# One decoder layer on one core: the conv taps of two units crossed on VectorE, and the scan's state made without a turn

## The reference

```python
xBC = causal_depthwise_conv(xBC, conv_w, conv_b)   # 4 taps over tokens, 4352 channels
...                                                 # x: 32 heads x 8; Bm, Cm: 32 heads x 64
CB = einsum('bcqhn,bckhn->bchqk', C, B)             # per chunk of 128 tokens and head
y_intra = einsum('bchqk,bckhp->bcqhp', CB * decay, xdt)
states = einsum('bckhn,bckhp->bchpn', B * state_decay[..., None], xdt)
new = carry * cd[:, :, None, None] + st             # state carried from chunk to chunk
y_inter = einsum('bcqhn,bchpn->bcqhp', C * exp(cum)[..., None], prev)
out = einsum('bli,oi->blo', y * silu(z + z_bias), W_out)
```

## Time and profile before

| | us |
|---|---|
| median of 3 runs (408.05 to 409.56) | 409.38 |
| profiled execution | 407.46 |
| its span | 405.7 |
| PE busy in the span | 381.7 (94%) |
| PE weight loads | 293.6 (72%) |
| DVE busy | 333.0 (82%) |
| ACT busy | 227.4 (56%) |
| POOL busy | 176.5 (43%) |

### The profile page before, as it was taken

How to read it: one execution, slowest core, us unless ns; L and a number is a source line. 1 busy time by engine, 2 the same in 40 slices (tenths; PEclk the granted TensorE clock), 3 DMA queues, 4 the chain that set the end, 5 groups by cost and what they waited for, 6 DMA issues and landing times.

```text
span 405.7 us, 8807 instructions
## 1 busy us (share of the span) xinstructions
PE 381.7 (94%) x2975; PEld 293.6 (72%) x2975; DVE 333.0 (82%) x564; ACT 227.4 (56%) x422; POOL 176.5 (43%) x208
## 2 busy tenths in 40 slices
PE   2998999999999999997899999899999999999996
PEld 1776776766767667665666676568888888888886
DVE  5798899999999999997889949748958759696685
ACT  7756555565564655657766731584554545546541
POOL 3897411101111011105536750235586755867561
PEclk9999999999999999998999999999999999999999
DMA  7302221322220122214231150000102020100003
GB/s 207 92 6 53 65 62 36 87 57 62 62 56 16 54 61 63 59 30 115 61 95 40 47 159 10 2 0 2 56 23 78 2 78 9 69 2 0 2 1 105
DMA packets 35932, 21.13 MB, mean 52 GB/s; under 512 B 17048, under 2 KB 33760, under 8 KB 35904
## 3 DMA queue, kind: packets, MB, share of 16 engines
q1 hardware_dynamic: 35904, 20.78, 18.4%
HBM read 18.13 MB, written 1.31 MB: 48 GB/s over the span
## 4 chain that ended last, share of the span: by engine, by line
PE 67%; DVE 15%; ACT 7%; issue 6%; POOL 2%; DMA 1%; ACTq 0%; DVEq 0%; SPq 0%; POOLq 0%
PE bank L1275 22%; PE bank L1251 9%; PE bank L1241 9%; PE bank L1469 8%; PE bank L1244 4%; PE bank L1389 3%; DVE conv L1013 3%; PE bank L1261 2%; PE bank L1457 2%; DVE conv L1220 2%; PE bank L1416 2%; ACT conv L687 1%; POOL el L648 1%; PE bank L1477 1%; DVE xres L1199 1%
## 5 line engine op out<-in xcount | busy, mean ns | idle before, releaser
L1013 DVE SCALAR_TENSOR_TENSOR conv<-bank,taps,conv 128x510 f32<-128x510 f32 (+2 forms) x204 | 149.7, 745 | 18.9 <-ACT conv L687 13.8
L1275 PE MATMUL bank<-uth,parts 128*128 128x512 f32 x272 | 96.4, 412 | 0.8 <-DVE conv L1013 0.7
L687 ACT ACTIVATE conv<-bank,tap_b,taps 128x512 f32<-128x512 f32 x68 | 52.9, 779 | 70.4 <-PE bank L1275 61.9
L561 POOL TENSOR_TENSOR ce<-conv,ecx 128x512 f32<-128x512 f32 x15 | 19.4, 1293 | 120.6 <-DVE conv L1013 120.6
L1275 PEld LDWEIGHTS bank<-uth,parts 128*128 128x128 f32 x272 | 51.7, 190 | 19.1 <-issue 3.3
L643 POOL TENSOR_TENSOR ul<-conv,uh 128x512 fp32r<-128x512 f32 x32 | 42.9, 1358 | 38.6 <-ACT uh L914 25.6
L648 POOL TENSOR_TENSOR el<-conv,parts 128x512 fp32r<-128x512 f32 x30 | 44.3, 1501 | 30.3 <-ACT parts L926 30.3
L1275 PE MATMUL bank<-utl,parts 128*128 128x512 f32 x136 | 54.1, 398 | 0.0
L1208 DVE CAST uh<-conv 128x512 fp32r<-128x512 f32 x28 | 26.0, 967 | 22.5 <-ACT conv L910 22.1
L1098 DVE SCALAR_TENSOR_TENSOR g<-dec,bank 128x512 f32<-128x512 f32 x64 | 40.8, 679 | 0.0
L1220 DVE TENSOR_TENSOR conv<-conv 128x512 f32<-128x512 f32 x32 | 31.4, 1014 | 10.4 <-ACT conv L931 10.3
(11 more groups left out here) (204 smaller groups left out, 730.7 us busy)
## 6 DMA issues: line engine op xcount, KB each, us to landing
w_raw<-in_L_attn_W_in_dram SPq DMA_DIRECT2D x17, 256.0 KB, 3.3
ecx<-ecum_dram SPq DMA_DIRECT2D x32, 128.0 KB, 2.9
ew_raw<-in_L_ffn_Wup_dram SPq DMA_DIRECT2D x7, 256.0 KB, 2.9
ew_raw<-in_L_ffn_Wgate_dram SPq DMA_DIRECT2D x7, 256.0 KB, 3.2
ew_raw<-in_L_ffn_Wdown_dram SPq DMA_DIRECT2D x7, 256.0 KB, 4.6
xres<-in_x_dram SPq DMA_DIRECT2D x2, 512.0 KB, 4.1
out_dram<-xres SPq DMA_DIRECT2D x4, 256.0 KB, 2.2
yi<-yev SPq DMA_DIRECT2D x56, 16.0 KB, 1.8
```

The costliest lines, as they stand in the source:

```text
L687: act.activation(conv[q][:, j, HALF * h:HALF * (h + 1)], bank[u % 2][:], ACT.Identity, bias=tap_b[q][:, j:j + 1], scale=taps[q][:, j, TAPS ...
L1013: dve.scalar_tensor_tensor(out=dst[:, :, d:SEQ], in0=src[:, :, 0:SEQ - d], scalar=taps[q][:, j, TAPS - 1 - d:TAPS - d], in1=dst[:, :, d:SE ...
L1275: ins = pe.matmul(bank[u % 2][:], w, x_t, start=(i == 0), stop=(i == 3 * KD - 1))
```

## The change

`new_state` swaps its operands: `btok` (128 columns for each sequence) is loaded as weights and 16 columns of `xs` move. The result is already the turned state, in `bank[6]` from column 128 on, 32 columns apart for the sequences, where `copy_state` reads it. `turn_state`, `copy_state_turned` and the tile `stT` go. ACT's `copy_state(n)` moves from the start of pair n+1 to after `decays(n, 3)`, where `copy_state_turned` was. On DVE the taps of two units are interleaved: with (unit, tap), the order is (0,1) (0,2) (1,1) (0,3) (1,2) (1,3), and the same for units 2 and 3. The taps of unit 3 of pair n+1 thus come at the end of pair n. `taps_by` gives the count of `tap_done` at which a unit is done: 4, 6, 10, 12 in a pair in place of 3, 6, 9, 12, and PE's and POOL's waits use it. Pairs 0 and 1, made ahead of the loop, keep the old order.

```diff
@@ -266,6 +264,11 @@
         def last(n, ahead):
 
             return isinstance(n, int) and n + ahead > PAIRS
+
+        def taps_by(m, u):
+
+            in_turn = isinstance(m, int) and m < 2
+            return 12 * m + ((3, 6, 9, 12) if in_turn else (4, 6, 10, 12))[u]
 
         def over_experts(eng, body):
 
@@ -800,14 +803,8 @@
             def copy_b(n):
 
                 act.wait_ge(b_turned, n)
-                at_least(act, stT_done, n - 1)
+                at_least(act, st_done, n - 1)
                 act.copy(btok[:].rearrange("p b k -> p (b k)"), bank[6][:]).then_inc(b_read, 1)
-
-            def copy_state_turned(n):
-
-                act.wait_ge(stT_done, n)
-                at_least(act, st_done, n - 1)
-                act.copy(stT[:], bank[6][:, 0:P]).then_inc(stT_read, 1)
 
             def copy_state(n):
 
@@ -841,8 +838,6 @@
                     return
                 m, km, r = n + 1, k + (q + 1) // 2, 1 - q
                 first = isinstance(n, int) and n == 1
-                if not first:
-                    copy_state(n - 1)
                 decays(n, 0)
                 decays(n, 1)
                 if not first:
@@ -859,18 +854,16 @@
                 copy_b(n)
                 decays(n, 2)
                 decays(n, 3)
-                copy_state_turned(n)
+                copy_state(n)
                 beside(n, m, km, r, 2)
                 beside(n, m, km, r, 3)
 
             def last_pair(n):
 
-                copy_state(n - 1)
                 decays(n, 0)
                 decays(n, 1)
                 evacuate_y(n - 1, PAIRS // 2 - 1, 1)
                 copy_b(n)
-                copy_state_turned(n)
                 decays(n, 2)
                 copy_state(n)
                 decays(n, 3)
@@ -1019,6 +1012,21 @@
                 dve.wait_ge(x_in[t // 4], 16)
                 return xres[:, t, :]
 
+            def crossed_taps(m, q, v):
+
+                done = 12 * m + 3 * v
+                for i, (u, d) in enumerate(((v, 1), (v, 2), (v + 1, 1), (v, 3), (v + 1, 2), (v + 1, 3))):
+                    j, h = u // 2, u % 2
+                    src = bank[u % 2][:].rearrange("p (b l) -> p b l", b=2)
+                    dst = conv[q][:, j, HALF * h:HALF * (h + 1)].rearrange("p (b l) -> p b l", b=2)
+                    if d == 1:
+                        dve.wait_ge(acc_first, 4 * m + u + 1)
+                    else:
+                        dve.wait_ge(tap_done, done + (0, 1, 0, 2, 3, 5)[i])
+                    dve.scalar_tensor_tensor(
+                        out=dst[:, :, d:SEQ], in0=src[:, :, 0:SEQ - d], scalar=taps[q][:, j, TAPS - 1 - d:TAPS - d],
+                        in1=dst[:, :, d:SEQ], op0=ALU.mult, op1=ALU.add).then_inc(tap_done, 1)
+
             dve.memset(carry[:], 1.0)
             moments(0, range(T), from_x, mv_done)
             inverse_roots(slice(0, T), 1)
@@ -1085,12 +1093,12 @@
                 for u in range(4):
                     a, b = 4 * (n - 1) + u, u % 2
                     if u == 0:
-                        other_taps(n, q, 3)
+                        if isinstance(n, int) and n == 1:
+                            other_taps(n, q, 3)
                         if not last(n, 2):
                             rest_w(n + 2, q)
                     if u == 2 and not last(n, 1):
-                        other_taps(n + 1, 1 - q, 0)
-                        other_taps(n + 1, 1 - q, 1)
+                        crossed_taps(n + 1, 1 - q, 0)
                     dve.wait_ge(exp_done, a + 1)
                     dve.wait_ge(cb_done, 2 * (n - 1) + u // 2 + 1)
                     at_least(dve, y_done, a - 1)
@@ -1098,7 +1106,7 @@
                     dve.scalar_tensor_tensor(out=g[b][:], in0=dec[b][:], scalar=1.0, in1=bank[2 + b][:],
                                              op0=ALU.min, op1=ALU.mult).then_inc(g_done, 1)
                     if u == 3 and not last(n, 1):
-                        other_taps(n + 1, 1 - q, 2)
+                        crossed_taps(n + 1, 1 - q, 2)
                     if u == 1 and isinstance(n, int) and n == PAIRS:
                         gate_last(0)
                     if u == 3 and isinstance(n, int) and n == 1:
@@ -1269,7 +1277,10 @@
                         pe.wait_ge(wtl_done, m + 1)
                     if isinstance(m, int) and m == 0 and u < 2:
                         pe.wait_ge(utl_done, 2 * u + 2)
-                    at_least(pe, tap_done, 3 * (4 * m + u - 1))
+                    if u >= 2:
+                        pe.wait_ge(tap_done, taps_by(m, u - 2))
+                    elif not (isinstance(m, int) and m == 0):
+                        pe.wait_ge(tap_done, taps_by(m - 1, u + 2))
                 w = (wth, wth, wtl)[i % 3][q][:, j, k, :]
                 x_t = (uth, utl, uth)[i % 3][:, k, HALF * h:HALF * (h + 1)]
                 ins = pe.matmul(bank[u % 2][:], w, x_t, start=(i == 0), stop=(i == 3 * KD - 1))
@@ -1395,13 +1406,8 @@
                 pe.wait_ge(b_read, n)
                 pe.wait_ge(xp_done, n)
                 for b in range(NSEQ):
-                    ins = pe.matmul(bank[6][32 * b:32 * (b + 1), 0:P], xs[q][:, b, :], btok[:, b, :], start=True, stop=True)
-                ins.then_inc(stT_done, 1)
-
-            def turn_state(n):
-
-                pe.wait_ge(stT_read, n)
-                pe.transpose(bank[6][:, P:2 * P], stT[:], ident[:]).then_inc(st_done, 1)
+                    ins = pe.matmul(bank[6][:, P + 32 * b:P + 32 * b + 2 * HD], btok[:, b, :], xs[q][:, b, 0:2 * HD], start=True, stop=True)
+                ins.then_inc(st_done, 1)
 
             def from_state(n, h):
 
@@ -1460,7 +1466,7 @@
 
             def b_dot_c(n, q, h):
 
-                pe.wait_ge(tap_done, 12 * n + (9, 12)[h])
+                pe.wait_ge(tap_done, taps_by(n, 2 + h))
                 at_least(pe, g_done, 4 * (n - 1) + 2 * h)
                 for i in range(4):
                     s = slice((4 * h + i) * P, (4 * h + i + 1) * P)
@@ -1509,7 +1515,6 @@
 
             def end_pair(n, k, q):
 
-                turn_state(n - 1)
                 weigh(n - 1, 1 - q, 2)
                 exponents(n, k, q, 0)
                 exponents(n, k, q, 1)
@@ -1539,7 +1544,6 @@
                 exponents(n, k, q, 2)
                 exponents(n, k, q, 3)
                 project_out(range(1, 2))
-                turn_state(n)
                 b_dot_c(n, q, 1)
                 from_state(n, 0)
                 weigh(n, q, 1)
```

More of the change, by code:

```diff
@@ L128, in decoder_layer @@
         xs = [sb(f"xs{i}", [P, NSEQ, 32]) for i in range(2)]
-        stT = sb("stT", [P, P])
         btok = sb("btok", [P, NSEQ, P])
@@ L232, in decoder_layer @@
         b_turned, b_read, st_done, st_read = sem("b_turned"), sem("b_read"), sem("st_done"), sem("st_read")
-        stT_done, stT_read = sem("stT_done"), sem("stT_read")
         inter_done, ce_done, y_read = sem("inter_done"), sem("ce_done"), sem("y_read")
@@ L582, in decay_c_half @@
                     pool.wait_ge(inter_done, n - 1)
-                pool.wait_ge(tap_done, 12 * n + 9 + 3 * h)
+                pool.wait_ge(tap_done, taps_by(n, 2 + h))
                 b = slice(2 * h, 2 * h + 2)
@@ L1423, in residual @@
                 if t < 2:
-                    pe.wait_ge(tap_done, 12 * PAIRS + 9 + 3 * t)
+                    pe.wait_ge(tap_done, taps_by(PAIRS, 2 + t))
                 elif t < 4:
```

## The result

| | before | changed |
|---|---|---|
| median, us | 409.34 (4 runs, 408.05 to 409.56) | 415.32 (4 runs, 415.11 to 416.65) |
| profiled execution / its span | 407.46 / 405.7 | 416.65 / 414.9 |
| PE, PE loads, DVE busy | 381.7, 293.6, 333.0 | 392.3, 305.1, 327.9 |

The changed kernel takes 1.0185 times as long, 95% interval 1.0147 to 1.0223, where 416.4 us (+1.7%) was forecast. DVE does 5 us less and PE 11 more.

What follows compares the result with a forecast made beforehand. PE's own order was taken to set the pair; 0.4 + 5.0 - 0.7 - 0.5 + 2.2 + 0.65 = +7.0 us on the profiled 407.46 gave 414.5, and 416.4 (+1.7%) for the median, range 410.5 to 420.

Steps and rivals of the forecast that it cites:

- Eight loads of 0.11: In `new_state` on PE, eight float32 loads of 128 columns take 0.11 us each, 0.89 in all.
- PE's own pair of 12.80: PE's queue in a steady pair: 12.45 + 0.67 for later projections - 0.12 - 0.20 = 12.80 us.
- The way over four taps: From `b_dot_c` over unit 2's later projections and four DVE taps to the next `b_dot_c`: 13.0 us a pair.
- The wait of 0.2 at `b_dot_c`: In steady pairs PE, ready at 12.80, waits 0.2 us at `b_dot_c` for unit 2's fourth tap.
- the one at `from_state`: PE's wait at `from_state` for ACT's copy of the state goes, saving 0.20 us a steady pair.
- DVE was to be idle near 1.2 us a pair: Listed sign of a right forecast: DVE idle near 1.2 us in pairs of 13.0.
- DVE's work for 12.08 us: DVE's work in an old steady pair, 12.45 - 0.37 = 12.08 us, falling to 11.6 with the crossing.
- For pair 12 the term: In pair 12 unit 2's last tap waits for ACT's first tap of unit 3, 0.7 later: pair 0.7 us shorter.
- I took back 1.0 for the fourth tap: In pair 13 a wait of 1.5 us goes, the fourth tap takes back about 1.0: -0.5.
- faster: Rival: DVE is the bound, so pairs follow its 0.48 us less, -7.2 in all, 402.2 us; chance 0.08.
- cheap loads: Rival: 128 columns load in 0.062 us in `new_state`, as in the turns: +1.5 us, 410.9; chance 0.16.
- loads that don't overlap: Rival: each `new_state` load waits for the matmul before it, 1.6 us for eight: 426.9 us; chance 0.06.

Runs made afterwards that it cites:

- the state alone: Changed kernel with the taps back in turn (`taps_by` 3, 6, 9, 12), keeping the new way to make the state: 412.36 us, 1.0107 of the kernel before.
- the crossing alone: Changed kernel with `stT`, `turn_state` and the old `new_state` put back, taps left crossed: 408.23 us, 1.0011 of the kernel before.
- the doubled products: Changed kernel with each of the four new-state products made twice in a row: 431.94 us, 1.0585 of the kernel before.

## Why the prediction was right

Its main steps came out one by one. Eight loads of 0.11: 0.89 us between the loads of two stages, and 0.89 for eight more. PE's own pair of 12.80: 12.79 in the state alone. The way over four taps, 13.0 us: 12.99 in nine pairs and 13.01 and 12.98 in pairs 14 and 15, where it had to be the same although PE has less to do; 12.30 for it without the later projections (12.35 by my sum). The wait of 0.2 at `b_dot_c` and the end of the one at `from_state` are in the timeline. At pair 3, by the start of its loads, the changed kernel is 65.88 - 65.45 = 0.43 behind (0.4 forecast), from there to pair 12 another 4.9 (5.0), in pairs 14 and 15 2.2 (2.2), in the last pair 251.38 - 239.36 against 243.81 - 232.45, 0.66 (0.65).

One sign was off: DVE was to be idle near 1.2 us a pair, and waits 1.5. The prediction took DVE's work for 12.08 us, the old pair less its one wait, where the earlier trace rows have it busy for 11.79; and its own 13.0 less 11.6 is 1.4. No term of the sum was made from the 12.08.

The signs held in pairs 12 and 13, the sizes didn't. Pair 12 is 16.87 (199.68 less 182.81) against 17.33, -0.46 for -0.7; pair 13 is 13.69 against 13.83, -0.14 for -0.5. For pair 12 the term was ACT's first tap of unit 3, taken 0.7 later: it ended 0.9 later against the pair's start (198.19 - 182.81 = 15.38 for 191.98 - 177.51 = 14.47). For pair 13 I took back 1.0 for the fourth tap and didn't count that the crossing lets the router's split run behind all taps, beside GpSimd. Together 0.6 us too much hope.

That makes +6.9 at pair 16 and +7.6 behind the loop for +7.0. The 1.6 us on top in the profiled execution are a second stretch of half clock, behind the loop (columns as above: the changed kernel, then the kernel before, the same 27 matmuls):

```profile
270.55:277.45 6.90, 6.90 (x27) 5.70 (x28) 1.45 (x3) 4.18 (x6) 0.00 (x0) 0.75 0.00 0
```

```profile
262.98:268.29 5.31, 5.31 (x27) 4.31 (x28) 1.36 (x3) 4.08 (x6) 0.00 (x0) 1.00 0.00 0
```

Of the rivals, "faster" is refuted by the crossing alone, "cheap loads" by the doubled products, and loads that don't overlap by the 0.111 from load to load, under matmuls that are recorded at 0.26: that rival had 1.6 us for eight, and they take 0.89. The medians differ by 6.0 us and not 7.6: the kernel before ran from 406.3 to 409.9 us in all its runs, and one stretch of half clock more or less is 1.6. Each execution's mean granted clock, in the runs of that kernel made beside the experiments, bears this out in part: with 0.990 to 0.992 the kernel before took 409.2 to 409.9 us (13 runs), with 0.994 to 0.996 407.3 to 408.4 (15 runs), with 0.998 or 0.999 406.3 to 406.6 (11 runs) or 408.2 to 408.4 (6 runs, not explained). At like clock the changed kernel is some 7 us behind: 416.65 at 0.991, 415.1 to 415.4 at 0.995 and 0.996. So the forecast of the median came out within 1.1 us partly by luck: it put the median 1.9 above the profiled execution, where it lies 1.3 below it.

## What to carry to other kernels

Count a matmul by its weight load when few columns move: a float32 product is two loads here, and with 128 weight columns each load cost 0.11 us whether 16 or 32 columns moved; four narrow ones side by side with 128 moving, plus a turn, were cheaper (pairs of 12.45 with the turn where it was, 12.24 with it early, 12.79 without it). Before interleaving chains to save an engine time, ask who waits for the first of them to end, and what other edit lengthens the same way: here one part cost nothing, the other 1.1%, both 1.9%. A wait can be removed by moving its producer to a place between stages of its own shape in place of doing without it; here that was worth 0.9%.

## What was not expected of the hardware

A small VectorE operation between float32 tiles of 8 rows (0.42 us) took 1.48 us when GpSimd's product of 128x512 had started 0.10 before it, and ended 0.28 behind that; it was 1.46 to 1.48 in all five profiles with the taps of units 2 and 3 crossed and this split behind them, each time with that product started just before it, and 0.42 in the eight others, where none was running as it began. The rounding ahead of it shows the same more weakly: 0.28 in the six profiles in which GpSimd ran no such product as it began, and 0.40 to 0.43 in the seven in which one was running.

TensorE fell to half clock (0.50, 1.2 GHz) soon after it had stood: in pair 12 of the kernel before at 187.61, after 2.2 us of idle time for `btok` up to 186.20, and in the changed kernel behind the loop, after 1.5 us for the layer norm up to 270.55. Whether such a stretch comes changes from kernel to kernel though the work there is the same, at 1.6 us each (15.95 against 14.38 in pair 12, where the one that kept its clock had stood 2.2 us for `btok` as well).
